# Graph attention and mixture of experts on one core: the maxima of the experts' weights move from GpSimd to TensorE and VectorE, and one staging buffer serves W1 and W2

## What is computed

```python
xh = (x @ W).reshape(N, H, D)
e = leaky_relu(a_src[src] + a_dst[dst], NEG_SLOPE)
alpha = softmax of e over the edges of each dst
out = jax.ops.segment_sum(xh[src] * alpha[:, :, None], dst, num_segments=N).reshape(N, H * D) + bias
out = batchnorm(out) * gamma + beta + x            # x = x + this
...
probs = softmax(xt @ Wr + br);  top_p, top_idx = top_k(probs, 2)
xe = layernorm(xt)[None] * ln_g[:, None, :] + ln_b[:, None, :]
h = gelu(einsum('end,edh->enh', xe, W1) + b1[:, None, :])    # W1: 8 x 256 x 1024
y = einsum('enh,ehd->end', h, W2) + b2[:, None, :]           # W2: 8 x 1024 x 256
out = (weights[:, :, None] * sel).sum(axis=1)                # x = x + this
```

## Time and profile before

| | us |
|---|---|
| runs of the kernel before | 1912.76, 1914.09, 1914.47 |
| median | 1914.09 |
| the profiled execution, its own time | 1913.94 |
| span of its trace (first to last instruction) | 1912.1 |
| edge stage, from the first gather to the end of the last | 85.2 to 1193.5 |
| from the last gather to the first statistics of batch norm | 1193.5 to 1204.8 |
| batch norm, routing, experts | 1204.8 to 1912.1 |

### The profile page before, as it was taken

One profiled execution on the slowest core, in us unless ns is written; L12 is line 12 of the kernel. 1 busy time (PEld: TensorE's weight loads), 2 busy tenths in 40 slices (PEclk: granted clock), 3 DMA queues, 4 the chain that ended last, 5 costly groups with the idle time before them and its releaser, 6 DMA issues.

```text
span 1912.1 us, 37628 instructions
## 1 busy us (share of the span) xinstructions
PE 1678.6 (88%) x10798; PEld 1169.3 (61%) x10798; DVE 1393.0 (73%) x3802; ACT 1106.8 (58%) x2386; POOL 1213.9 (63%) x1157
## 2 busy tenths in 40 slices
PE   7678898998988989888899888846999999999997
PEld 5445554554544545445454444634999899998996
DVE  6686877877778777787778879897666666666664
ACT  3555676766667766676667765773443434434443
POOL 1377777777777777777777777202566566665553
PEclk9889999999999999999999999976999999999999
DMA  8655446455554555645555444592323333333232
GB/s 280 214 147 145 123 142 166 119 156 158 141 166 120 155 157 143 166 121 152 159 144 157 131 127 119 193 345 103 49 47 54 49 49 52 49 52 52 47 45 33
DMA packets 124147, 240.41 MB, mean 126 GB/s; under 512 B 25065, under 2 KB 82997, under 8 KB 122773
## 3 DMA queue, kind: packets, MB, share of 16 engines
q0 software_dynamic: 62800, 147.76, 32.8%
q1 hardware_dynamic: 51816, 80.51, 12.8%
q10 hardware_dynamic: 9340, 9.73, 1.5%
HBM read 195.47 MB, written 43.30 MB: 125 GB/s over the span
## 4 chain that ended last, share of the span: by engine, by line
PE 42%; POOL 26%; DVE 12%; issue 11%; DMA 7%; ACT 1%; DVEq 1%; POOLq 0%; ACTq 0%; SPq 0%
POOL gather_ring L1136 26%; PE bank L2068 14%; PE bank L2085 14%; PE bank L1263 6%; DMA gather_ring<-node_table,src_slot 4%; PE bank L1229 4%; DVE acc L1160 1%; PE bank L720 1%; PE bank L2049 1%; PE bank L976 1%; ACT r_ring L1395 1%; DMA out_rows<-y,token_idx 1%; DVE gather_ring L1188 1%; DVE feat L1411 1%; DMA raw_idx<-src_pad,edge_tile_i 1%
## 5 line engine op out<-in xcount | busy, mean ns | idle before, releaser
L1136 POOL DMA_INDIRECT gather_ring<-node_table,src_slot x879 | 837.6, 953 | 268.2 <-issue 253.5
L1229 PE MATMUL bank<-ones 128*128 128x512 bf16 x1787 | 557.5, 391 | 72.8 <-ACT gather_ring L1304 61.1
L1263 PE MATMUL bank<-gather_ring,onehot 128*128 128x264 f32 x1758 | 564.2, 403 | 53.7 <-DVE gather_ring L1188 53.0
L1263 PEld LDWEIGHTS bank<-gather_ring,onehot 128*128 128x128 f32 x1758 | 290.7, 194 | 266.1 <-DVE gather_ring L1188 228.8
L1160 DVE TENSOR_TENSOR acc<-acc,bank 128x264 f32 x879 | 368.7, 419 | 17.6 <-PE bank L1263 15.1
L1188 DVE TENSOR_TENSOR gather_ring<-gather_ring,bank 128x256 f32<-128x256 f32 x879 | 360.2, 410 | 0.3 <-ACT bank L1303 0.3
L2158 POOL DMA_INDIRECT out_rows<-y,token_idx x105 | 200.6, 1911 | 220.9 <-DMA out_rows<-y,token_idx 159.7
L1229 PEld LDWEIGHTS bank<-ones 128*128 128x128 bf16 x1787 | 170.7, 100 | 219.2 <-issue 98.0
L2127 ACT ACTIVATE hid<-bank,cols 128x256 f32<-128x256 f32 (+1 forms) x448 | 210.4, 551 | 148.1 <-PE bank L2068 145.1
L2068 PE MATMUL bank<-xe,w_hi 128*128 128x256 f16 (+1 forms) x1792 | 285.3, 267 | 1.7 <-DVE xe L1990 1.5
L2085 PE MATMUL bank<-w,hid_hi 128*128 x1680 | 278.2, 273 | 0.0
(11 more groups left out here) (316 smaller groups left out, 1965.9 us busy)
## 6 DMA issues: line engine op xcount, KB each, us to landing
w_stage<-in_L_ffn_W SPq DMA_DIRECT2D x16, 1024.0 KB, 7.5
dst_row<-dst_rows SPq DMA_DIRECT2D x110, 128.0 KB
gather_ring<-node_table,src_slot POOLq DMA_INDIRECT x879
w_split<-w_out SPq DMA_DIRECT2D x32, 256.0 KB
w<-w_split SPq DMA_DIRECT2D x8, 1024.0 KB, 9.2
node_table<-acc ACTq DMA_DIRECT2D x24, 264.0 KB
r_ring<-in_x_lanes SPq DMA_DIRECT2D x7, 896.0 KB, 6.6
xt<-in_x_lanes SPq DMA_DIRECT2D x24, 256.0 KB, 5.0
```

Of the source, the lines that this page charges most:

```text
L1136: e.indirect_dma_start(out=gather_ring[:, b % GB, j, :], out_offset=None, in_=node_table, in_offset=bass.IndirectOffsetOnAxis(ap=src_slot[ ...
L1229: e.matmul(to[:, :].rearrange("p (k n) -> p k n", k=2), halves[:, 0:P], halves.rearrange("p (a n) -> p a n", a=1).broadcast_to([P, 2, 2 * ...
L1263: e.matmul(bank[AGG[s % len(AGG)]][:, 0:ROW], onehot[:, b % OHB, j, :], gather_ring[:, b % GB, j, :], start=True, stop=True).then_inc(summ ...
```

## The change

The two buffers become one, `stage`, and the 16 loads (W1 and W2 of eight experts) become 16 units that take turns in it: unit u is W1 for even u and W2 for odd u, it begins at batch 4 + 6 u and has six steps. The load still stands at step 0, so every load has the batch it had before. The largest values of the two halves are now taken at steps 1 and 2. The maximum over the partitions takes four operations: TensorE turns the column of 128 values into a row of `gained` (after its sums at step 2), VectorE reduces the row and multiplies the result with a piece of `ident` (step 3), TensorE multiplies this with ones, which spreads it over the partitions (after its sums at step 3), and VectorE copies it out of PSUM (step 4), followed by the same power of two as before. GpSimd has no part in it any more. ScalarE does two pieces per batch at steps 4 and 5, one before and one after `make_onehot`; VectorE does the low parts in the middle of the messages of steps 4 and 5, at the start of step 5 and at the start of the next unit's step 0. SyncE stores one piece at step 4, two at step 5, and the fourth at the next step 0, just ahead of the next load.

```diff
-        w1_stage = early.take("w1_stage", [P, KD, HID])
-        w2_stage = early.take("w2_stage", [P, KH * D])
+        stage = early.take("stage", [P, KD * HID])
+        w1_stage, w2_stage = stage[:, :].rearrange("p (k h) -> p k h", k=KD), stage
...
-        W1_AT, W2_AT, W_STEPS = GB, GB + 6, 12
-        MEASURE_AT, TOP_AT, HI_AT = 2, 8, 8
+        UNITS, UNIT_AT, UNIT_STEPS = 2 * NE, GB, 6
+        LOAD_AT, BIAS_AT, MEASURE_AT, SPREAD_AT, TOP_AT, HI_AT = 0, 2, 1, 3, 4, 4
...
-        COLUMNS_AT = W2_AT + (NE - 1) * W_STEPS + TOP_AT + 2
+        COLUMNS_AT = UNIT_AT + UNIT_STEPS * (UNITS - 1) + TOP_AT + 1
...
+            if step == LOAD_AT:
+                if u:
+                    store_w2(e, u - 1, PIECES - 1)
...
+                    e.wait_ge(hi_made, PIECES * u)
+                    e.wait_ge(lo_made, PIECES * u)
+                    e.wait_ge(bias_done, (u + 1) // 2)
+                if kind == 0:
+                    e.dma_start(w1_stage, W1[ee].rearrange("(k p) h -> p k h", p=P)).then_inc(unit_loaded, 16)
+                else:
                     e.dma_start(w2_stage[:, :].rearrange("p (c d) -> p c d", d=D),
+                                W2[ee].rearrange("(c p) d -> p c d", p=P)).then_inc(unit_loaded, 16)
+            if step == HI_AT:
+                store_w2(e, u, 0)
+            if step == HI_AT + 1:
+                store_w2(e, u, 1)
+                store_w2(e, u, 2)
...
-        def pool_weights(e, b):
-            ee, step = w1_step(b)
-            if step == TOP_AT and ee < NE:
-                e.wait_ge(w1_max_made, ee + 1)
-                e.partition_all_reduce(w1_top[:, ee, :], w1_max[:, ee, :], P,
-                                       bass.bass_isa.ReduceOp.max).then_inc(w1_top_made, 1)
...
+        def tensor_peaks(e, b):
...
+            if step == MEASURE_AT + 1:
+                e.wait_ge(max_made, u + 1)
+                e.transpose(gained[0:n, 0:P], unit_max[:, 0:n], ident[:, :]).then_inc(max_turned, 1)
+            if step == SPREAD_AT:
+                e.wait_ge(peaks_made, u + 1)
+                e.matmul(gained[:, PEAK_AT:PEAK_AT + n], ones[0:n, :], unit_peaks[0:n, 0:n], start=True, stop=True
+                         ).then_inc(peaks_spread, 1)
...
+        def vector_peaks(e, u):
+            n = 2 - u % 2
+            e.wait_ge(max_turned, u + 1)
...
+            vector_order.of(e.tensor_reduce(unit_peak[0:n, :], gained[0:n, 0:P], AX.X, ALU.max))
+            e.wait_ge(vector_order.sem, vector_order.n)
+            e.tensor_scalar(unit_peaks[0:n, 0:n], ident[0:n, 0:n], unit_peak[0:n, 0:1], None, ALU.mult).then_inc(peaks_made, 1)
...
         def pool_edges(e, batches):
             for b in batches:
-                pool_weights(e, b)
...
                     message(b, j)
                     if s >= ADDS_BEHIND:
                         add(*divmod(s - ADDS_BEHIND, EB))
+                    if j == EB // 2 - 1:
+                        vector_weights_between(e, b)
...
+                tensor_peaks(e, b)
                 if b + 2 < BATCHES:
                     picks(b + 2)
...
-                scalar_w1(e, b)
-                scalar_w2(e, b)
+                scalar_weights(e, b, 0)
                 if b + 1 < BATCHES:
                     make_onehot(b + 1)
+                scalar_weights(e, b, 1)
```

More of the change, by code:

```diff
@@ L910, in gain_of, with sync_weights @@
             return vecs[:, NE * KH:NE * (KH + KD)].rearrange("p (x c) -> p x c", c=KD)[:, :, k]
-        def sync_w1(e, b):
-            ee, step = w1_step(b)
-            if step == 0 and ee < NE:
-                if ee == 0:
+        def sync_weights(e, b):
+            u, step = unit_step(b)
+            if not 0 <= u <= UNITS:
+                return
+            if step == LOAD_AT:
+                if u:
+                    store_w2(e, u - 1, PIECES - 1)
+                if u == UNITS:
+                    return
+                kind, ee = kind_of(u)
+                if u == 0:
                     e.wait_ge(acc_started, GROUPS)
@@ L977, in tensor_w1_bias @@
                                         vecs[:, at:at + 1], start=(k == 0), stop=(k == KD - 1))
[L978 removed]
+                made.then_inc(bias_done, 1)
         def vector_w1_bias(e, b):
[L981 to L983 removed]
+            u, step = unit_step(b)
+            kind, ee = kind_of(u)
+            if step == BIAS_AT and 0 <= u < UNITS and kind == 0:
+                e.wait_ge(bias_done, ee + 1)
                 vector_order.of(e.tensor_tensor(expert_cols[:, ee, B1_COL:B1_COL + KH],
@@ new lines, in tensor_peaks @@
+        def tensor_peaks(e, b):
+            u, step = unit_step(b)
+            if not 0 <= u < UNITS:
+                return
+            n = 2 - u % 2
[6 more added lines that the diff above has]
+                         ).then_inc(peaks_spread, 1)
@@ L1088, in across, with vector_weights_between @@
+            if step == HI_AT + 1:
+                vector_lo(e, u, 1)
+        def vector_weights_between(e, b):
+            u, step = unit_step(b)
+            if 0 <= u < UNITS and HI_AT <= step < HI_AT + 2:
+                vector_lo(e, u, 2 * (step - HI_AT))
         def across(ap, n):
```

245 lines of the change are left out of this document (103 added, 142 removed).

## The result

Twenty runs of each kernel: before 1915.99 us (1912.14 to 1919.88), after 1911.94 us (1909.26 to 1914.48). The ratio is 0.9981, with an interval from 0.9974 to 0.9987: 3.6 us less. The forecast, 1910.6 us against the three runs of before with their median of 1914.09, was a ratio of 0.9982. The median after lies 0.14 us above my own range (1909.6 to 1911.8) and inside the range for 8 in 10; before itself read 1.9 us more in its twenty runs than in the first three. The profiled execution took 1911.39 us, 1909.0 of them in the span.

What follows compares the result with a forecast made beforehand. GpSimd's issuing of 879 gathers, 1.25 us each, was taken to bound the edge stage. 1913.94 less 3.5 for the maxima, other terms 0, gave 1910.4, with the median 0.15 above: 1910.6 us; 8 in 10: 1908.8 to 1914.3.

Steps and rivals of the forecast that it cites:

- What is removed: Edge stage, GpSimd: sixteen maxima over the partitions go, 0.22 us each on the gathers' pace, 3.5 us saved.
- What is added: Edge stage: small VectorE operations, 0.6 us per unit, and TensorE products, some 0.3 us; 0 on GpSimd's clock.
- the rival's 0.22 us: Edge stage: a small VectorE operation per unit holds a gather for 0.22 us, 3.5 us given back; within chance 0.16.
- What is moved: Edge stage: ScalarE's two pieces per batch, later loads and stores; lags stay inside the ring's slack, counted as 0.
- the bound on the lag: W1 loads: TensorE waits at most 9.4 us, then 3.7 us of bias products; 13.1 us at eight places.
- slack of 21.4 us: Gather ring of four batches: the engines behind can fall back 21.4 us before GpSimd has to wait.
- The end of the stage: Batches 104 to 108: VectorE's divisions hold four gathers; their changed phase gives -1.0 to +1.0 us, taken as 0.
- the replay: End of the edge stage, played through from batch 104: the holds sum to 4.0 to 4.6 us in place of 4.16.
- The 0.9 us that the last score could have gained: End of the edge stage: the last score starts 3.7 us after its gather; it gains 0.9 us if 2.8 suffices.
- rival 1: Edge stage: divisions hold gathers 1.9 us each, or small VectorE operations hold them; nothing gained, 1914.0 us, chance 0.16.
- rival 2: End of the edge stage: the four holds shrink to 0.65 us each, 1.6 us more gained; 1909.0 us, chance 0.15.
- What would show it: Signs in the changed kernel's profile: edge stage about 1105 us; wrong if the stages behind moved by more than 1 us.

Runs made afterwards that it cites:

- the ring of three: The changed kernel with a gather ring of three batches in place of four; 1916.42 us, 0.9999 of before.
- the probe: The changed kernel with one added VectorE operation of 1792 elements in every second batch from 12 to 98, four kinds in turn; 1933.67 us, only run.
- own_maxima_2: The kernel before without its sixteen maxima over the partitions, old staging kept; 1914.05 us, 0.9983 of before (1.0012 in its first run, on the slow chip).
- two_buffers_2: The changed kernel with two staging buffers again, each load issued at step 2 of the unit before; 1915.55 us, 0.9987 of before.

## Why the prediction was right

**What is removed: right.** 3.5 us were predicted, 3.52 stood in the trace of before, none in the one after, and 3.46 in the kernel that has them back. The medians agree: taken away alone they gave 3.3 us (1.5 to 4.8), put back alone they took the gain away. That the total came within 0.1 us of the forecast's ratio is partly luck: in the profiled pair the gathers gained 2.26 us only, and the stages behind, which the change doesn't touch, differed by 2.35 us; the ring of three, without maxima, showed no gain at all.

**What is added: right.** Groups by line of the kernel after, shapes apart, the new operations (busy us, mean ns | idle before):

```profile
L1057 DVE TENSOR_REDUCE unit_peak<-bank 1x1 f32<-1x128 f32 x8 | 2.2, 272 | 0.0
...
L1059 DVE TENSOR_SCALAR unit_peaks<-ident,unit_peak 1x1 f32<-1x1 f32 x8 | 1.6, 201 | 0.3
...
L1071 DVE COPY w_top<-bank 128x1 f32<-128x1 f32 x8 | 1.2, 151 | 0.0
```

That is 0.62 us for a unit of W2, whose rows these are, where 0.6 was taken. A unit of W1 took 0.67 us. No gather beside them took more than 0.99 us; the rival's 0.22 us for each didn't come.

**What is moved: the cover held, the bound on the lag didn't.** The bound was 13.1 us at eight places, 9.4 us of waiting for the load and 3.7 us of bias products, against a slack of 21.4 us. What GpSimd waits for is the last sum of a batch. In the kernel after it came latest in batch 89: its last gather, the end of its last sum, and the first gather of batch 93, which needs this sum:

```profile
987.48 0.95 POOL L1142 DMA_INDIRECT gather_ring<-node_table,src_slot  x1 [0.30 <-issue]
...
1009.90 0.61 PE L1270 MATMUL bank<-gather_ring,onehot 128*128 128x264 f32 x2
...
1018.82 0.94 POOL L1142 DMA_INDIRECT gather_ring<-node_table,src_slot  x1 [0.30 <-issue]
```

1018.82 less 1010.51 leaves 8.3 us of the 21.4, a lag of 13.1 us. That it equals the bound is chance, as the load took far less than its 9.4 us. Timeline of TensorE in the kernel after:

```profile
993.40 6.96 PE L973 MATMUL bank<-vecs,stage 128*128 128x1 f32 x32 [3.00 <-DMA stage<-in_L_ffn_W]
...
1000.53 4.01 PE L1236 MATMUL bank<-ones 128*128 128x512 bf16 x9
...
1010.64 2.10 PE L1236 MATMUL bank<-ones 128*128 128x512 bf16 x9
```

and its stretches around it:

```profile
975.00:990.00 15.00, 13.04 (x60) 7.05 (x60) 12.15 (x36) 12.35 (x27) 11.34 (x13) 1.00 0.73 206
990.00:993.40 3.40, 0.40 (x2) 0.03 (x1) 0.00 (x0) 0.00 (x0) 2.79 (x3) 0.88 0.85 285
993.40:1000.40 7.00, 7.00 (x37) 7.00 (x38) 2.03 (x5) 5.42 (x13) 5.17 (x7) 0.50 0.50 134
1000.40:1010.00 9.60, 9.60 (x39) 5.63 (x37) 6.66 (x21) 0.66 (x1) 7.16 (x8) 0.70 0.41 112
```

The wait for the load was 3.0 us, as long as the last part of the prediction said. But after these 3 us without work the granted clock, 1.00 until 990, was 0.50, the lower level of 1.2 GHz. The 32 products took 6.96 us in place of the 3.70 of the earlier trace rows, 3.26 us more, and the nine products behind the picks 4.01 us in place of 2.10, 1.9 us more. Added up as an estimate, the 13.1 us are 3.0 of waiting, 3.7 of bias products, 5.2 of the lower clock, and 1.2 that are left for the rest of these batches. No step of the prediction had the clock in its bound. It sufficed that the load lay far under its own bound. With the full 9.4 us the lag would have been 6.4 us more, by this estimate 19.5 us, and 1.9 us of the 21.4 would have been left. VectorE stood 4.73 us for the picks, and the score of batch 90 began 12.0 us after its last gather (997.49 to 1009.44) in place of 2.8. With two buffers the wait for the load is gone, the least slack left behind the first batch is 12.8 us, and GpSimd's longest wait is 0.3 us with either: the lag is the staging's doing and is paid out of the ring.

**The end of the stage: right in size, with a small miss in sign.** Timeline of GpSimd in the kernel after, the four held gathers, which answer to the earlier trace rows:

```profile
1150.20 1.71 POOL L1142 DMA_INDIRECT gather_ring<-node_table,src_slot  x1 [0.30 <-issue]
...
1158.48 2.65 POOL L1142 DMA_INDIRECT gather_ring<-node_table,src_slot  x1 [0.30 <-issue]
...
1172.70 1.93 POOL L1142 DMA_INDIRECT gather_ring<-node_table,src_slot  x1 [0.30 <-issue]
...
1182.44 2.14 POOL L1142 DMA_INDIRECT gather_ring<-node_table,src_slot  x1 [0.30 <-issue]
```

Their excess is 4.64 us against 4.17; the replay had said 4.0 to 4.6, and the term was taken as 0. The worst, 2.65 us, began 0.20 us after its division (1158.28). The 0.9 us that the last score could have gained did not come either: it starts at 1194.86, 3.74 us after the last gather, as before. Neither rival 1 (holds of 1.9 us each) nor rival 2 (0.65 us each) came true. The Trainium skill's rule, "SBUF — State Buffer", section "Who interferes with whom", was rightly left out of the sum: operations with two inputs in SBUF held the gathers in 11 of 11 cases, and with the second input in PSUM in none. What fails here is the page's inference, not its rule on two inputs: that rule is about GpSimd instructions that read SBUF, and a gather reads its row numbers from `src_slot`, which lies there. Which part of a gather is held no run here tells. On the other kinds the page agrees with the probe: by it a reduction never contends, and an operation with one input and a constant can, in its faster modes.

**What would show it.** Of the signs, these came: no maximum in the stage, steps of 1.25 us, no wait of GpSimd for TensorE above 0.3 us, a wait of 3.0 us before the bias products. VectorE's wait for gathers fell by 28.2 us where 10 to 25 were expected. I had put that at its added work, and taken this one wait alone. With its waits for sums and for picks added, the trace of before has 222.1 us and that of own_maxima_2, without any added work, 221.3; those with it have 204.5 (the change) and 204.2 (two_buffers_2). So with the added work there are some 17 us less of these waits, with late loads or without. The late loads only move 22 us from one wait to the others (192.7 to 170.2 us): a score that comes late finds its gathers landed. From the first gather to the end of the last it took 1106.0 us, not 1105. The stages behind moved by 2.35 us, more than the 1 us that I had named as a sign of error. That sign was chosen badly: on seven traces with the same instructions there they read 705.0 to 709.6 us.

**What stays open.** Why the plain steps and the stages behind differ between executions; why the kernel with a ring of three, 0.9999 of before (0.9989 to 1.001), shows none of the change's gain; and what made the first chip slow.

## What to carry to other kernels

Where an engine's own issuing sets the pace, a short instruction put between its steps costs what the distance between its neighbours grows by (0.22 us here), not its own duration (0.32 us), and it can be read off the trace to a few hundredths. Look next at what the other engines do to that issuer: four of VectorE's five divisions cost it more (4.2 us) than sixteen of its own instructions (3.5 us), and one operand in PSUM made that free. And before a gain of some microseconds is read from one pair of traces, compare the parts that the change can't have touched: here they moved by 2.35 us in one pair and by up to 4.6 us over seven traces, and the gain is 3.6.

## What the runs showed of the hardware

- The step between two gathers isn't the same in every execution: the mean of all steps of at most 1.30 us was 1.2506 to 1.2538 us in the seven traces from the faster chips that the two tables show, and 1.2500 and 1.2538 for one and the same kernel (own_maxima) in its two profiled executions, on two chips. 878 x 0.0032 = 2.8 us, nearly as much as the change.
- An indirect DMA on GpSimd that began during a VectorE operation of 1792 elements per partition was held when the operation had two inputs in SBUF (11 of 11), or one input and a constant (9 of 9), and not when it was a reduction or had the second input in PSUM. It then ended 0.8 us after the operation. Two gathers that began 0.16 us ahead of a scalar operation were held too (1.37 us) and ended 0.12 us after it; one that began 0.11 us ahead of a division was not (0.95 us).
- TensorE's granted clock, 1.00 before, was 0.50 after a stop of 3.0 us for a load, and 32 products of one column then took 1.9 times as long (6.96 against 3.70 us).
- From a batch's last gather to its score it took 2.8 us in quiet batches where before takes 1916 us, and 20 to 35 us on a chip where it takes 2197 us, though a gather's packets ended 2.4 to 2.5 us after its start on both. There GpSimd waited 125.3 us for the ring and 170.2 us for something unnamed, and no change to the issuing could be seen.
